# Attention output in split precision: one 128-column matmul a key chunk in place of three, with the parts added outside TensorE

## The chip, the cores and the metric

The kernel runs on one core of a Trainium2 chip. The metric is the device time in microseconds, taken as the median over runs. The core's engines are TensorE (PE, with its weight loads as PEld), VectorE (DVE), ScalarE (ACT), GpSimd (POOL) and SyncE (SP), which issues the transfers. Each engine works through its own instructions in program order and waits on semaphores for the others.

## The reference

A decoder with two layers works on x of shape (8, 100, 512) and a context of shape (8, 722, 512). Each layer has a mixing part, a cross attention over the context with 16 heads of 32 features, and a feed-forward part, each followed by a layer norm. The change touches the cross attention of both layers:

```python
q = split_heads(query @ Wq + bq)
k = split_heads(bank @ Wk + bk)
v = split_heads(bank @ Wv + bv)
scores = jnp.einsum('bhqd,bhkd->bhqk', q, k) / scale
attn = jax.nn.softmax(scores, axis=-1)
out = jnp.einsum('bhqk,bhkd->bhqd', attn, v)
out = out.transpose(0, 2, 1, 3).reshape(B, -1, D)
return out @ Wo + bo
```

The second layer's attention differs in having a mask over the keys and no biases on q, k and v. There are 8 batches, 100 queries (T) and 722 keys (KEYS) in each.

## The kernel before

Matmul operands are kept as two float32r parts, a high part and a low part that holds the rest, and each product is made by the helper `three` (lines 272 to 274): high by high, high by low, low by high, all added up in PSUM. ACT writes the high parts, DVE (or POOL) the low ones.

The keys of a batch are cut into six chunks of up to 128 (NKC = 6; the last has 82 rows). Attention handles one batch at a time, and within it one head a step: `batch` on PE runs steps t = 0 to 16, and DVE and ACT have a `batch` with the same steps. The order on each engine is written out by hand. In step t:

- PE: `scores(t)` into psS (one of two buffers), `transposes(t - 1)` of the exponentials into psT (a single buffer), then `weighted`, one half (three key chunks) of the product of probabilities and values for a pair of heads, into psO. In steps 0, 1, 4, 5, 8 and 9 it also projects a half of the next keys (`keys`), and in steps 15 and 16 those of the next batch.
- ACT: `probs_hi(t - 1)` (two copies of psT to pT.hi, line 615), then `exps(t)` (line 606), then whatever else the step has: a half of the keys (`keys_hi`), or in steps 10, 11, 13 and 14 the high part of the next batch's context (`context_hi`, line 565).
- DVE: `head_max(t)` (line 918; in the second layer lines 923 and 928), `probs_lo(t - 1)` (line 936), and in even steps from 4 on `heads_out` (line 947), which copies the two heads of a finished pair from psO to `oraw`.

The waits that tie the steps together: `exps(t)` waits for `head_max(t)`; `transposes(t)` waits for `exps(t)` and for `probs_lo(t - 1)`, as psT has one buffer; `weighted` of a pair waits for its low parts and for the `heads_out` of the pair before, as psO has one buffer. Steps 0 to 2 have no `weighted`.

Behind step 16 comes a tail: the values of the next batch (`values`, six times 12 matmuls) with the last pair's `weighted` between the first two of them, and on DVE the scaling of `oraw` by the reciprocal sums (line 978), in the first layer a bias (line 982), then the split into oT and the output projection. Below, "a step with keys" is one in which PE also runs `keys`.

## Time and profile before

| | |
|---|---|
| device time, median of 3 runs | 2616.84 us (2612.31 to 2621.23) |
| span of the profiled execution, first to last instruction | 2613.8 us |
| share of the span in which PE was busy | 93% |
| DVE, ACT, POOL | 42%, 36%, 22% |
| the chain that ended last, share on PE | 86% |
| mean granted TensorE clock | 0.934 |

The page gives the profiled execution by its span alone; the median of the runs is 3.0 us above it. The first layer's attention covers some 109 to 757 us of the span, the second layer's some 1131 to 1787. Matmul ends are modelled, so that PE's speed is read from the starts of successive matmuls and not from their durations. A wait is shown at the end of a row in brackets, with what ended it.

### The profile page before, as it was taken

To read this page: it belongs to the slowest core of one execution; us is meant where nothing else is said; L and a number is where in the kernel's file an instruction comes from. 1 tells how busy PE (TensorE), PEld (TensorE's weight loads), DVE (VectorE), ACT (ScalarE), POOL (GpSimd) and SP (SyncE) were. 2 spreads that over 40 slices of the span, in tenths; PEclk is the share of its full clock that TensorE was granted. 3 is DMA by queue.
4 is the path that set the end of the run, shared out by engine and by line. 5 is a ranking of instruction groups with operands and counts; after the bars stand their busy time and mean duration, and the time that the engine had idled before them with its cause. 6 is when DMAs were issued, how large, how long until landed. Compare 5 with 4: busy or idle time off the path is not lost.

```text
span 2613.8 us, 38193 instructions
## 1 busy us (share of the span) xinstructions
PE 2432.4 (93%) x14208; PEld 2160.2 (83%) x14208; DVE 1110.8 (42%) x2206; ACT 947.7 (36%) x1892; POOL 585.1 (22%) x397
## 2 busy tenths in 40 slices
PE   4899999999977789699999999998999999999997
PEld 3788888888866667588888888887999999999997
DVE  7455545555457368444556455654640000200022
ACT  2444434454443144343454344533222222311130
POOL 4111101110132634311111011101222222222222
PEclk9899999999978878789999999998999999999998
DMA  3000000000021010100100000000111111111111
GB/s 136 1 24 24 15 8 23 23 23 6 22 81 29 1 44 0 60 1 28 28 27 21 6 27 27 32 1 33 64 48 65 56 64 56 56 56 64 56 57 41
DMA packets 29513, 93.60 MB, mean 36 GB/s; under 512 B 3752, under 2 KB 4008, under 8 KB 29320
## 3 DMA queue, kind: packets, MB, share of 16 engines
q1 hardware_dynamic: 29448, 92.72, 11.0%
q8 instruction: 42, 0.69, 0.1%
q14 instruction: 23, 0.19, 0.0%
HBM read 91.07 MB, written 1.64 MB: 35 GB/s over the span
## 4 chain that ended last, share of the span: by engine, by line
PE 86%; DVE 6%; ACT 3%; POOL 3%; issue 2%; DMA 0%; DVEq 0%; SPq 0%; POOLq 0%; ACTq 0%
PE psS L272 18%; PE psS L274 16%; PE psS L273 16%; PE psT L1337 7%; PE psJ L272 4%; PE psJ L273 4%; PE psJ L274 4%; PE psO L272 4%; PE psO L274 3%; PE psO L273 3%; PE psT L272 2%; PE psT L274 2%; PE psT L273 2%; DVE x_res L884 1%; DVE stats L877 1%
## 5 line engine op out<-in xcount | busy, mean ns | idle before, releaser
L272 PE MATMUL psS<-hid_hi,fw_hi 128*128 128x400 f32 x1152 | 398.1, 346 | 15.4 <-DVE hid_lo L1258 10.6
L274 PE MATMUL psS<-hid_hi,fw_lo 128*128 128x400 f32 x1152 | 400.2, 347 | 0.0
L273 PE MATMUL psS<-hid_lo,fw_hi 128*128 128x400 f32 x1152 | 399.6, 347 | 0.0
L529 POOL TENSOR_TENSOR fw_lo<-raw,fw_hi 128x1024 fp32r<-128x1024 f32 x88 | 216.7, 2464 | 572.1 <-ACT fw_hi L751 572.1
L615 ACT ACTIVATE pT_hi<-psT 128x300 fp32r<-128x300 f32 x512 | 187.4, 418 | 263.0 <-PE psT L1337 262.5
L1258 DVE TENSOR_TENSOR hid_lo<-h_act,hid_hi 128x800 fp32r<-128x800 f32 x32 | 32.3, 1083 | 555.6 <-ACT hid_hi L840 555.6
L606 ACT ACTIVATE p<-psS,nmax 100x722 f32<-100x722 f32 x256 | 221.9, 867 | 68.9 <-DVE nmax L928 36.4
L936 DVE TENSOR_TENSOR pT_lo<-psT,pT_hi 128x300 fp32r<-128x300 f32 x512 | 216.4, 464 | 38.1 <-ACT pT_hi L615 32.8
L370 POOL TENSOR_TENSOR cT_lo<-ctx_raw,cT_hi 128x722 fp32r<-128x722 f32 x58 | 102.1, 1761 | 580.0 <-ACT cT_hi L565 580.0
L272 PEld LDWEIGHTS psS<-hid_hi,fw_hi 128*128 128x128 f32 x1152 | 218.0, 189 | 16.4 <-issue 11.2
L272 PE MATMUL psO<-pT_hi,vv_hi 128*64 128x200 f32 (+1 forms) x768 | 219.2, 285 | 2.4 <-DVE oraw L947 2.4
L272 PE MATMUL psJ<-cT_hi,wk_hi 128*128 128x362 f32 (+1 forms) x512 | 184.4, 360 | 38.3 <-POOL cT_lo L370 16.9
L274 PEld LDWEIGHTS psS<-hid_hi,fw_lo 128*128 128x128 f32 x1152 | 219.4, 190 | 0.0
L273 PEld LDWEIGHTS psS<-hid_lo,fw_hi 128*128 128x128 f32 x1152 | 218.0, 189 | 0.0
L1337 PE MATMUL psT<-ident,p 100*128 100x100 f32 x1536 | 198.6, 269 | 12.1 <-ACT p L606 12.1
L274 PE MATMUL psO<-pT_hi,vv_lo 128*64 128x200 f32 (+1 forms) x768 | 206.4, 269 | 0.0
L273 PE MATMUL psO<-pT_lo,vv_hi 128*64 128x200 f32 (+1 forms) x768 | 205.8, 268 | 0.0
L272 PE MATMUL psS<-kT_hi,qs_hi 32*100 32x512 f32 (+1 forms) x512 | 191.2, 373 | 4.6 <-POOL qs_lo L375 4.6
L1337 PEld LDWEIGHTS psT<-ident,p 100*128 100x128 f32 x1536 | 149.1, 147 | 42.9 <-DVE pT_lo L936 9.8
L273 PE MATMUL psJ<-cT_lo,wk_hi 128*128 128x362 f32 (+1 forms) x512 | 176.7, 345 | 0.0
L274 PE MATMUL psJ<-cT_hi,wk_lo 128*128 128x362 f32 (+1 forms) x512 | 175.8, 343 | 0.0
L273 PE MATMUL psS<-kT_lo,qs_hi 32*100 32x512 f32 (+1 forms) x512 | 169.3, 331 | 0.0
(306 smaller groups left out, 4909.4 us busy)
## 6 DMA issues: line engine op xcount, KB each, us to landing
raw<-ffn_dram SPq DMA_DIRECT2D x88, 512.0 KB, 3.2
ctx_raw<-ctxT_dram SPq DMA_DIRECT2D x60, 361.0 KB, 3.1
mask_raw<-mask_dram SPq DMA_DIRECT2D x8, 282.0 KB
raw<-wk_dram SPq DMA_DIRECT2D x4, 512.0 KB, 3.5
raw<-wv_dram SPq DMA_DIRECT2D x4, 512.0 KB, 6.6
raw<-wq_dram SPq DMA_DIRECT2D x4, 512.0 KB, 3.3
raw<-wo_dram SPq DMA_DIRECT2D x4, 512.0 KB, 3.2
cin<-xT_dram SPq DMA_DIRECT2D x1, 1600.0 KB, 8.3
```

Source lines behind the costliest of these rows:

```text
L272: nc.tensor.matmul(out, st[0], mv_[0], start=first, stop=False)
L273: nc.tensor.matmul(out, st[0], mv_[1], start=False, stop=False)
L274: return nc.tensor.matmul(out, st[1], mv_[0], start=False, stop=last)
L370: nc.gpsimd.tensor_tensor(cT.lo[:, c, :], src[:, c % 2, :], cT.hi[:, c, :], ALU.subtract)\
L529: nc.gpsimd.tensor_tensor(fw.lo[:, e, :], raw[:, e, :], fw.hi[:, e, :], ALU.subtract)\
L606: nc.scalar.activation(p[:, h % 2, 0:KEYS], psS[h % 2][0:T, 0:KEYS], ACT.Exp, bias=nmax[:, h % 2:h % 2 + 1], accum_out=rsum[:, h:h + 1]).t ...
L615: nc.scalar.activation(pT.hi[:, pr % 2, HK * i:HK * i + HK, (h % 2) * T:(h % 2 + 1) * T], psT[:, KA * i:KA * i + HK * T].rearrange("p (k t ...
L877: nc.vector.bn_stats(stats[:, s, :], src).then_inc(ln_stat, 1)
L884: nc.vector.tensor_scalar(x_res[:, b, :], src, mv[:, s, 0:1], rstd[:, s, :], ALU.subtract, ALU.mult).then_inc(ln_x, 1)
L936: nc.vector.tensor_tensor(pT.lo[sl], psT[:, KA * i:KA * i + HK * T].rearrange("p (k t) -> p k t", k=HK), pT.hi[sl], ALU.subtract).then_inc ...
L1258: nc.vector.tensor_tensor(hid.lo[:, k % M, :], h_act[:, k % M, :], hid.hi[:, k % M, :], ALU.subtract)\
L1337: mm = nc.tensor.transpose(psT[:, k0:k0 + T], p[:, h % 2, KC * k:KC * (k + 1)], ident[0:T, 0:T])
```

## The change

The two parts of the values, formerly two tensors, lie beside each other head by head in one tensor `vv`, so that for two heads 128 consecutive columns hold (head 0 high, head 0 low, head 1 high, head 1 low), 32 each. The two parts of the probabilities `pT` lie beside each other for each chunk, high for 2 x 100 queries and then low. One matmul a chunk multiplies all with all: 128 stationary columns, 400 moving ones. psO then holds every combination apart. What is wanted for head e is its rows of high values under the high and the low probabilities, and its rows of low values under the high ones. DVE adds the first two while it takes them out (a `tensor_reduce` over two elements in place of a copy), ACT copies the third to a new tensor `ocross` on the partitions of `oraw` (new `heads_cross`), and once a batch DVE adds `ocross` to `oraw`.

```diff
-        vv = pair("vv", [P, NKC, D])
+        vv = at("vv", [P, NKC, H, 2, HD], f32r)
...
-        pT = pair("pT", [P, 2, NKC, 2 * T])
+        pT = at("pT", [P, 2, NKC, 2, 2 * T], f32r)
...
+        ocross = at("ocross", [P, C, T], fp32)
...
+                def heads_cross(b, pr):
+
+                    act.wait_ge(a.pv_mm, H // 2 * b + pr + 1)
+                    if pr == 0:
+                        wait(act, a.o_summed, b)
+                    for e in range(2):
+                        g, j = divmod(2 * pr + e, G)
+                        cp = nc.scalar.activation(ocross[HD * j:HD * (j + 1), g, :],
+                                                  psO[2 * HD * e + HD:2 * HD * (e + 1), T * e:T * (e + 1)], ACT.Copy)
+                    cp.then_inc(a.o_crossed, 1)
...
                         if t < H:
                             exps(b, t)
+                        if t >= 4 and t % 2 == 0:
+                            heads_cross(b, (t - 4) // 2)
...
                         queries_hi(a, b + 1)
                         values_hi(a, b + 1, 0)
+                    heads_cross(b, H // 2 - 1)
+                    if not last:
                         values_hi(a, b + 1, 1)
...
                     for e in range(2):
                         g, j = divmod(2 * pr + e, G)
-                        cp = nc.vector.tensor_copy(oraw[HD * j:HD * (j + 1), g, :],
-                                                   psO[HD * e:HD * (e + 1), T * e:T * (e + 1)])
+                        r = slice(2 * HD * e, 2 * HD * e + HD)
+                        cp = nc.vector.tensor_reduce(oraw[HD * j:HD * (j + 1), g, :],
+                                                     psO[r, 0:4 * T].rearrange("p (s x t) -> p x t s", s=2, x=2)[:, e],
+                                                     AX.X, ALU.add)
...
+                    dve.wait_ge(a.o_crossed, H // 2 * (b + 1))
+                    dve.wait_ge(a.o_copied, H // 2 * (b + 1))
+                    nc.vector.tensor_tensor(oraw[:, :, :], oraw[:, :, :], ocross[:, :, :], ALU.add)\
+                      .then_inc(a.o_summed, 1)
                     dve.wait_ge(a.rb_mm, b + 1)
-                    dve.wait_ge(a.o_copied, H // 2 * (b + 1))
+                    dve.wait_ge(a.o_summed, b + 1)
...
                         wait(pe, a.o_copied, H // 2 * b + pr)
-                    fs = slice(2 * HD * pr, 2 * HD * (pr + 1))
+                        wait(pe, a.o_crossed, H // 2 * b + pr)
                     for k in range(HK * half, HK * (half + 1)):
                         n = key_rows(k)
-                        mm = three(psO[0:2 * HD, 0:2 * T], (vv.hi[0:n, k, fs], vv.lo[0:n, k, fs]),
-                                   (pT.hi[0:n, pr % 2, k, :], pT.lo[0:n, pr % 2, k, :]), k == 0, k == NKC - 1)
+                        mm = nc.tensor.matmul(psO[:, 0:4 * T],
+                                              vv[0:n, k, 2 * pr:2 * pr + 2, :, :].rearrange("p h s e -> p (h s e)"),
+                                              pT[0:n, pr % 2, k, :, :].rearrange("p s t -> p (s t)"),
+                                              start=k == 0, stop=k == NKC - 1)
```

What the change does to the instructions is seen in three places. The first is PE in a step without keys in the first layer: scores into psS, transposes into psT, then the half pair of `weighted` into psO (the last figure is rows of the output x moving columns). Before:

```order
L274 MATMUL psS<-kT_hi,qs_lo 100x512
L272 MATMUL psS<-kT_hi,qs_hi 100x210
L273 MATMUL psS<-kT_lo,qs_hi 100x210
L274 MATMUL psS<-kT_hi,qs_lo 100x210
L1337 MATMUL psT<-ident,p 128x100 x6
L272 MATMUL psO<-pT_hi,vv_hi 64x200
L273 MATMUL psO<-pT_lo,vv_hi 64x200
L274 MATMUL psO<-pT_hi,vv_lo 64x200
```

Now:

```order
L275 MATMUL psS<-kT_hi,qs_lo 100x512
L273 MATMUL psS<-kT_hi,qs_hi 100x210
L274 MATMUL psS<-kT_lo,qs_hi 100x210
L275 MATMUL psS<-kT_hi,qs_lo 100x210
L1360 MATMUL psT<-ident,p 128x100 x6
L1371 MATMUL psO<-pT,vv 128x400 x3
L273 MATMUL psS<-kT_hi,qs_hi 100x512
```

The last three rows of before stand twice more behind each other, and are not repeated. These nine matmuls of 200 columns into 64 rows became three of 400 columns into 128 rows; nothing else on PE moved. The second place is ACT in steps 10 to 12 of the first batch: exponentials of a head (p), the context's high part (cT_hi), the probabilities' high part (pT). Before:

```order
L606 ACTIVATE p,rsum<-psS,nmax 100x722
L565 ACTIVATE cT_hi<-ctx_raw 128x722
L615 ACTIVATE pT_hi<-psT 128x3x100 x2
L606 ACTIVATE p,rsum<-psS,nmax 100x722
L565 ACTIVATE cT_hi<-ctx_raw 128x722
L615 ACTIVATE pT_hi<-psT 128x3x100 x2
L606 ACTIVATE p,rsum<-psS,nmax 100x722
```

Now:

```order
L608 ACTIVATE p,rsum<-psS,nmax 100x722
L629 ACTIVATE ocross<-psO 32x100 x2
L566 ACTIVATE cT_hi<-ctx_raw 128x722
L617 ACTIVATE pT<-psT 128x3x100 x2
L608 ACTIVATE p,rsum<-psS,nmax 100x722
L566 ACTIVATE cT_hi<-ctx_raw 128x722
L617 ACTIVATE pT<-psT 128x3x100 x2
L608 ACTIVATE p,rsum<-psS,nmax 100x722
L629 ACTIVATE ocross<-psO 32x100 x2
```

The two copies stand behind the exponentials of every even step, and in step 10 (and 14) ahead of the context's part. The third place is DVE in the tail of the first batch, from the reciprocals on. Before:

```order
L969 RECIPROCAL rinv<-rsum 100x16
L908 TENSOR_TENSOR vv_lo<-psS,vv_hi 128x512 x2
L947 COPY oraw<-psO 32x100 x2
L908 TENSOR_TENSOR vv_lo<-psS,vv_hi 128x512
L978 TENSOR_TENSOR oraw<-psT,oraw 128x400
L982 TENSOR_TENSOR oraw<-oraw,cols 128x400
L908 TENSOR_TENSOR vv_lo<-psS,vv_hi 128x512
```

Now:

```order
L988 RECIPROCAL rinv<-rsum 100x16
L925 TENSOR_TENSOR vv<-psS,vv 128x16x32 x2
L965 TENSOR_REDUCE oraw<-psO 32x100 x2
L925 TENSOR_TENSOR vv<-psS,vv 128x16x32
L997 TENSOR_TENSOR oraw<-oraw,ocross 128x400
L1001 TENSOR_TENSOR oraw<-psT,oraw 128x400
L1005 TENSOR_TENSOR oraw<-oraw,cols 128x400
L925 TENSOR_TENSOR vv<-psS,vv 128x16x32
```

The addition of `ocross` stands ahead of the scaling, and the copies out of psO are reductions now, here as in every even step.

## Rows read from the trace of the kernel before

**Rows 1.** Page: the span, and the granted clock in 40 slices.

```profile
span 2613.8 us, 38193 instructions
...
PEclk9899999999978878789999999998999999999998
```

**Rows 2.** Windows over a batch: length, busy time of each engine, clock.

```profile
279.00:364.00 85.00, 84.40 (x526) 70.54 (x525) 43.96 (x87) 37.16 (x86) 10.08 (x8) 0.94 0.06 17
532.70:613.20 80.50, 79.90 (x526) 66.40 (x525) 44.08 (x87) 37.27 (x87) 10.10 (x8) 1.00 0.06 18
```

**Rows 3.** Timeline, second layer, a step without keys: start, length, engine, instruction.

```profile
1267.03 0.73 PE L1337 MATMUL psT<-ident,p 100*128 100x100 f32 x6
...
1267.29 0.92 DVE L923 CUSTOM_DVE_ANT_0 psS<-psS,maskb 100x722 f32<-100x722 f32 x1 [0.65 <-PE psS L274]
...
1267.54 0.31 PE L272 MATMUL psO<-pT_hi,vv_hi 128*64 128x200 f32 x1
...
1267.80 0.73 ACT L615 ACTIVATE pT_hi<-psT 128x300 fp32r<-128x300 f32 x2 [0.27 <-PE psT L1337]
...
1268.41 0.85 DVE L936 TENSOR_TENSOR pT_lo<-psT,pT_hi 128x300 fp32r<-128x300 f32 x2
...
1268.49 0.87 ACT L606 ACTIVATE p<-psS,nmax 100x722 f32<-100x722 f32 x1
...
1269.25 0.19 ACT L606 ACTIVATION_READ_ACCUMULATOR p<-psS,nmax 100x1 f32 x1
...
1269.29 0.52 DVE L947 COPY oraw<-psO 32x100 f32<-32x100 f32 x2
...
1269.69 0.73 PE L1337 MATMUL psT<-ident,p 100*128 100x100 f32 x6
```

**Rows 4.** Timeline of PE, second layer, the tail's six chunks of `weighted`, then `values`.

```profile
1279.26 0.25 PE L272 MATMUL psO<-pT_hi,vv_hi 128*64 128x200 f32 x1
...
1280.92 0.42 PE L272 MATMUL psS<-wv_hi,cT_hi 128*128 128x512 f32 x1
```

**Rows 5.** Timeline of PE, feed-forward, two matmuls that stand 20 apart.

```profile
2100.14 0.34 PE L272 MATMUL psS<-hid_hi,fw_hi 128*128 128x400 f32 x1
...
2103.78 0.34 PE L274 MATMUL psS<-hid_hi,fw_lo 128*128 128x400 f32 x1
```

**Rows 6.** Timeline of PE, first layer, `transposes(0)`, `transposes(1)`, then two chunks.

```profile
277.60 0.73 PE L1337 MATMUL psT<-ident,p 100*128 100x100 f32 x6
...
280.08 1.21 PE L1337 MATMUL psT<-ident,p 100*128 100x100 f32 x6 [0.60 <-ACT p L606]
...
281.59 0.37 PE L272 MATMUL psO<-pT_hi,vv_hi 128*64 128x200 f32 x1
...
282.09 0.37 PE L272 MATMUL psO<-pT_hi,vv_hi 128*64 128x200 f32 x1
```

**Rows 7.** Timeline of PE, second layer, the same two transposes of another batch.

```profile
1307.44 0.73 PE L1337 MATMUL psT<-ident,p 100*128 100x100 f32 x6
...
1309.98 0.73 PE L1337 MATMUL psT<-ident,p 100*128 100x100 f32 x6 [0.67 <-ACT p L606]
```

**Rows 8.** Single lines: count, shortest/median/longest in ns, first and last start.

```profile
L947 DVE COPY oraw<-psO x256: 237/254/260, 121.9 to 1778.7; 32x100 f32<-32x100 f32 x128
...
L1169 DVE TENSOR_REDUCE gsum<-gsq x8: 676/680/685, 946.1 to 1051.9; 100x16 f32<-100x512 f32 x8
...
L644 ACT ACTIVATE rT<-psT x16: 227/228/243, 169.6 to 1778.5; 16x100 f32<-16x100 f32 x16
...
L982 DVE TENSOR_TENSOR oraw<-oraw,cols x8: 574/575/576, 173.9 to 756.7; 128x400 f32<-128x400 f32 x8
```

**Rows 9.** Timeline of ACT, first layer, behind the context's part of step 10.

```profile
237.82 0.73 ACT L615 ACTIVATE pT_hi<-psT 128x300 fp32r<-128x300 f32 x2 [0.38 <-PE psT L1337]
```

**Rows 10.** Timeline of DVE, second layer, the tail, behind the scaling.

```profile
1291.53 0.69 DVE L908 TENSOR_TENSOR vv_lo<-psS,vv_hi 128x512 fp32r<-128x512 f32 x1 [2.90 <-ACT vv_hi L599]
```

**Rows 11.** Windows at the start of a batch, columns as in rows 2.

```profile
280.10:290.30 10.20, 10.20 (x46) 9.33 (x47) 3.04 (x6) 3.15 (x8) 0.00 (x0) 0.50 0.00 0
```

More of the change, by code:

```diff
@@ L232, in decoder_kernel @@
                               "qs_hi qs_done s_mm maxed exped t_mm pt_hi pt_lo pv_mm o_copied rinv_done rt_mm "
-                              "rt_copied rb_mm o_scaled "
+                              "rt_copied rb_mm o_scaled o_crossed o_summed "
                               "o_biased o_hi o_lo resid_done mask_in mask_done pad_done") for L in range(2)]
@@ L598, in values_hi @@
                 n = key_rows(j)
-                nc.scalar.activation(vv.hi[0:n, j, :], psS[j % 2][0:n, 0:D], ACT.Copy).then_inc(a.v_hi, 1)
+                nc.scalar.activation(vv[0:n, j, :, 0, :], psS[j % 2][0:n, 0:D].rearrange("p (h e) -> p h e", h=H),
+                                     ACT.Copy).then_inc(a.v_hi, 1)
             def attention(L):
@@ L615, in probs_hi @@
                         nc.scalar.activation(
-                            pT.hi[:, pr % 2, HK * i:HK * i + HK, (h % 2) * T:(h % 2 + 1) * T],
+                            pT[:, pr % 2, HK * i:HK * i + HK, 0, (h % 2) * T:(h % 2 + 1) * T],
                             psT[:, KA * i:KA * i + HK * T].rearrange("p (k t) -> p k t", k=HK), ACT.Copy)\
                           .then_inc(a.pt_hi, 1)
+                def heads_cross(b, pr):
[7 more added lines that the diff above has]
+                    cp.then_inc(a.o_crossed, 1)
                 def batch(b, last):
@@ L907, in values_lo @@
                 n = key_rows(j)
-                nc.vector.tensor_tensor(vv.lo[0:n, j, :], psS[j % 2][0:n, 0:D], vv.hi[0:n, j, :], ALU.subtract)\
-                  .then_inc(a.v_lo, 1)
+                nc.vector.tensor_tensor(vv[0:n, j, :, 1, :], psS[j % 2][0:n, 0:D].rearrange("p (h e) -> p h e", h=H),
+                                        vv[0:n, j, :, 0, :], ALU.subtract).then_inc(a.v_lo, 1)
             def attention(L, base):
@@ L934, in probs_lo @@
                         dve.wait_ge(a.pt_hi, 2 * (H * b + h) + i + 1)
-                        sl = (slice(None), pr % 2, slice(HK * i, HK * i + HK), slice((h % 2) * T, (h % 2 + 1) * T))
-                        nc.vector.tensor_tensor(pT.lo[sl],
+                        ks, ts = slice(HK * i, HK * i + HK), slice((h % 2) * T, (h % 2 + 1) * T)
+                        nc.vector.tensor_tensor(pT[:, pr % 2, ks, 1, ts],
                                                 psT[:, KA * i:KA * i + HK * T].rearrange("p (k t) -> p k t", k=HK),
-                                                pT.hi[sl], ALU.subtract).then_inc(a.pt_lo, 1)
+                                                pT[:, pr % 2, ks, 0, ts], ALU.subtract).then_inc(a.pt_lo, 1)
                 def heads_out(b, pr):
```

## The prediction, made before the changed kernel was run

> **What bounds the kernel now.** I read the page first: a span of 2613.8 us and a granted TensorE clock at or near full nearly everywhere [rows 1]. Attention is what the change touches, so I cut it into batches with the windows. A batch takes 85.0 us at a mean clock of 0.94, of which PE is busy 84.4; one batch takes 80.5 at clock 1.00, with the same 526 matmuls [rows 2]. DVE (44 us) and ACT (37) are busy for half of that. So PE bounds the batch as a whole, and the clock is worth some 4.5 us of it. The share of a batch is still an average, and what a shorter PE is worth must be read stage by stage.
>
> The timeline of a step without keys shows the other limit close by. From one set of transposes to the next is 1269.69 - 1267.03 = 2.66 us, and PE does not wait [rows 3]. But the exponentials that release the next transposes end at 1269.25 + 0.19 = 1269.44, only 0.25 us ahead of them. The reader is to see a ring: transposes, 0.77 later the high parts on ACT (1267.80), behind them the exponentials (1268.49), 0.95 to their end, and the next transposes. DVE has little room either: from its maximum at 1267.29 to the end of its copies at 1269.81 are 2.52 us in this even step.
>
> How fast the ring turns when PE is not in its way can be read off directly, in step 2, where PE has no `weighted` to do: transposes to transposes is 280.08 - 277.60 = 2.48 us in the first layer, with PE waiting 0.60 for ACT [rows 6], and 1309.98 - 1307.44 = 2.54 in the second, waiting 0.67 [rows 7]. I take these as the floor of a step.
>
> **What PE saves.** Six chunks of three 200-column matmuls take 1280.92 - 1279.26 = 1.66 us, 0.277 a chunk [rows 4]. A matmul of the new shape, 128 stationary by 400 moving columns, is the feed-forward's: twenty of them in 2103.78 - 2100.14 = 3.64 us, 0.182 each, weight loads hidden [rows 5]. That is 0.095 a chunk and 0.28 us a half pair of three chunks. Both prices are from long undisturbed runs of the same instruction forms, so the term is tight. The Trainium skill (VectorE: DVE Perf Modes, the TRN2 errata section) gives a matmul 6 cycles more than its columns; by that a chunk would save 0.088 us and the whole sum would be some 2 us smaller, and the rows above are slower than it for either shape.
>
> A batch has 16 half pairs: one in each of steps 3 to 16, and two in the tail.
>
> - PE is the bound in the steps with keys (4, 5, 8, 9, 15, 16) and in the tail. There all 0.28 comes out: 8 half pairs. A ninth is step 3, which stands in the stretch at half clock at the batch's start [rows 11], where PE is slower and so the bound: a chunk there takes 282.09 - 281.59 = 0.50 us [rows 6]. Its saving at that clock is larger (the new matmul costs at most twice 0.182, so 0.14 a chunk), but the stretch at half clock lasts as long as before and takes in other work instead, so I count it at 0.28. Sum 9 x 0.284 = 2.56 us.
> - Steps 6, 7, 10, 11, 12, 13 and 14 have no keys. PE would need 2.66 - 0.28 = 2.38, less than the floor. In the first layer they come down to 2.48 (0.18 each), in the second to 2.54 (0.12 each): 1.26 and 0.84 us.
>
> **What the additions cost.** *DVE*: a copy of 100 elements takes 0.254 us and a short-run reduction of 512 elements 0.680 [rows 8]. On the line between them (1.03 ns an element) the new reduction of 200 costs 0.36, so a pair goes from 0.52 to 0.72. The bounds are 0.254 (as the copy) and 0.68. The Trainium skill (VectorE: DVE Perf Modes, Rules for kernel authors) calls `tensor_reduce` the slowest DVE operation and advises against it on a hot path; by its "1x" the price is again one element a cycle, which the reduction's row agrees with, so it gives the same 0.36.
>
> Does DVE then bound the second layer? The chain over two steps, from one set of transposes: 0.77 to the high parts, some 0.42 for the first half of these, on which the low parts wait, 0.85 for the low parts, 0.72 for the reductions, 1.20 from the maximum's start to the exponentials' (1268.49 - 1267.29), 0.95 for these and some 0.15 for semaphores: 5.06 us [rows 3]. Two floors of 2.54 are 5.08. It is a tie, so I leave 2.54, but it has no slack: each 0.1 us more on a reduction lengthens a pair of steps by 0.2.
>
> *ACT*: two copies of 32x100 cost about as much as the 0.228 us of the nearest row [rows 8], 0.36 to 0.46 a pair. They stand behind the exponentials of even steps, where ACT otherwise idles until the next transposes (0.77 us are needed for them), so they are hidden. In steps 10 and 14 the context's part of the next batch is there too. ACT waited 0.38 us behind it at a step of 2.66 [rows 9]; at 2.48 some 0.20 is left, and 0.4 must fit in. I charge 0.2 twice a batch. If that cover were absent altogether, the copies would cost 0.4 in each of seven steps, 2.8 us a batch.
>
> The copies also stand in front of the next pair's `weighted`, as the reductions do: both end about when its transposes do. I charge nothing; the wait would take the place of the ring's.
>
> *Tail*: the addition of `ocross` is like the bias, 0.575 us [rows 8], and the last reductions 0.2. Behind the scaling DVE waits 2.90 us for the next batch's values [rows 10], and PE is busy with these. Hidden in seven batches; in the last batch of a layer nothing covers it, at most 0.8 us, 1.6 for both. I take 1. The new layouts of `vv` and `pT` have the same element counts and runs of 32 and 100 elements; I take no cost.
>
> **The sum.** First layer 2.56 + 1.26 - 0.40 = 3.42 us a batch, second 2.56 + 0.84 - 0.40 = 3.00; eight batches each: 27.4 + 24.0 = 51.4, less 1 for the ends of the layers: 50 us. Span 2613.8 - 50 = 2564; the runs' median stood 3.0 above the span, so 2567 us.
>
> **Rival 1: the clock falls more often.** At the start of a batch the clock goes to half for 10.2 us [rows 11], right after steps 1 and 2, in which PE did only 32-row scores and transposes and waited 0.60 us [rows 6]. One batch had the same wait and no fall [rows 2], so this stretch is near whatever decides. The change makes the steps without keys more like it: of 2.66 us they now spend 0.83 on `weighted`, afterwards 0.55 of 2.48 to 2.54, and PE waits 0.1 to 0.2 us in each; in steps 10 to 14 five of them stand in a row. If the clock falls there, for the same 10.2 us, it costs about what it costs now at the start, 4.5 us (85.0 - 80.5). Once a batch in the second layer: 36 us, leaving 14, 2603. The Trainium skill (TensorE: Matmul & The Clock Gate, What's actually happening) says that the clock follows how busy the array has been lately, which speaks for this rival. Against it: the new matmuls use all 128 columns and never leave PE idle for as much as 0.6. Chance 0.17.
>
> **Rival 2, the other side: the same fall in both layers.** Once a batch in 16 batches is 72 us against the 50 saved: 2639, slower. It decides from 0.7 falls a batch on. What speaks for it is that batches are alike, so that a fall that happens in one is likely to happen in most. Chance 0.14.
>
> **Rival 3: DVE or ACT becomes the bound.** With reductions of 0.5 us (the strided read of PSUM, two elements 200 apart, has no row), a pair of steps in the second layer is 5.06 + 0.28 = 5.34, as long as before (2 x 2.66), so that the 0.8 goes: 2573. At the upper bound of 0.68 it is 5.7: seven steps lose 0.19 each instead of gaining 0.12, in all 2.2 us a batch, and at most as much in the first layer: 35 us, 2602. Chance 0.13.
>
> **Rival 4: more than forecast.** If the matmul that fills the array keeps the clock up at the batch's start, 4.5 us in most of 16 batches comes on top: 2567 - 60 = about 2505; in part of them, 2540. Chance 0.1. That the change doesn't do what it says I exclude: the instruction order shows three matmuls where nine were.
>
> **How the numbers follow.** The forecast has 0.46: 2567, with a range of its own of 2552 to 2582 (floor of a step 0.1 lower or higher in 112 steps is 11 us, the ACT term 3, the tail 1). A measurement here tells some 0.3% from no change, 2609 to 2625. Faster: the forecast, rivals 3 and 4, and most of rival 1: 0.78. Slower: rival 2 with the upper half of what could come on top of it, 0.14. Within 0.3%: 0.08, from rival 1 with a few falls in the first layer too. The range must reach over rivals 3 and 1 and to the partial case of rival 4, and leaves out rival 2: 2543 to 2612.
>
> **What the profile would show.** The starts of two matmuls of line 1371 0.18 us apart at full clock. Transposes to transposes in steps 6 to 14 without keys 2.48 in the first and 2.54 in the second layer, now with a wait of PE for ACT. Line 965 at 0.36 us, line 629 at 0.23. A batch at 81.5 us in the first layer with one stretch at half clock. A second such stretch in steps 10 to 14 would show rival 1 or 2; a PE wait for the maximum of DVE, or a longer line 965, rival 3. The prediction is wrong if the steps with keys do not shorten by 0.28, or if the clock does something else than before.

## The result: 61 us slower, where 50 us faster was forecast

The changed kernel takes 2679.51 us (median of 4 runs, 2664.34 to 2687.57), the kernel before beside it 2618.20 us (4 runs, 2612.31 to 2621.23). The ratio is 1.0225 [1.0189, 1.0261]. Here and below medians are over all runs of a kernel and ratios over its fast runs alone, so that the two can differ where the runs spread. The forecast was 2567 with a range of 2543 to 2612; what came is rival 2, and more of it than its 2639.

The page of the changed kernel (profiled run 2664.34 us), for [rows 1]:

```profile
span 2662.5 us, 35459 instructions
...
PE 2463.9 (93%) x12672; PEld 2144.8 (81%) x12672; DVE 1148.7 (43%) x2222; ACT 1012.1 (38%) x2148; POOL 583.6 (22%) x397
...
PEclk9789899879888778788889898988999999999998
```

PE is as busy as before, 93%, with 1536 matmuls fewer. The clock row tells why: in attention (slices 3 to 12 and 18 to 28) there are 8s and 7s in most places where 9s were. The mean granted clock went from 0.934 to 0.897. The windows of one whole batch of the first layer, of a row of its steps at full clock, and of the steps behind it:

```profile
281.67:369.93 88.26, 86.77 (x430) 69.94 (x429) 46.27 (x88) 41.44 (x101) 10.05 (x8) 0.86 0.06 17
...
303.94:325.60 21.66, 21.00 (x129) 16.61 (x129) 15.61 (x31) 15.05 (x38) 3.18 (x2) 1.00 0.04 7
325.60:339.30 13.70, 13.70 (x52) 11.30 (x51) 6.52 (x13) 7.37 (x20) 3.77 (x3) 0.50 0.32 98
```

A batch has 96 matmuls fewer than in [rows 2] and takes 88.3 us in place of 85.0, at a clock of 0.86. Beside the stretch at half clock at its start [rows 11] it has a second one, of 13.7 us, in steps 12 to 15. Stretches are counted here and below in the trace's record of the granted clock: those that begin between the first transposes of a layer's attention and 12 us behind its last ones. There are 15 before (143 us) and 32 after (341 us).

What the change costs on the other engines, single lines, for [rows 8] (line 965 is the reduction, 629 ScalarE's copy):

```profile
L965 DVE TENSOR_REDUCE oraw<-psO x256: 343/360/367, 128.7 to 1827.1; 32x100 f32<-32x200 f32 x128
...
L629 ACT ACTIVATE ocross<-psO x256: 242/246/250, 124.6 to 1827.0; 32x100 f32<-32x100 f32 x128
```

The first is as forecast, 0.36 us. The second is a little longer, 0.246 us for 0.23, and a pair of copies takes 0.50 (below) where 0.36 to 0.46 was forecast. What both do to the steps was not forecast. Three places of the timeline show it; in each row the figures are start and length. First ScalarE in the step of the first layer in which a part of the context stands behind the copies, for [rows 9]:

```profile
320.37 0.50 ACT L629 ACTIVATE ocross<-psO 32x100 f32<-32x100 f32 x2
...
320.48 0.73 PE L1360 MATMUL psT<-ident,p 100*128 100x100 f32 x6
...
320.90 0.81 ACT L566 ACTIVATE cT_hi<-ctx_raw 128x722 fp32r<-128x722 f32 x1
...
321.73 0.73 ACT L617 ACTIVATE pT<-psT 128x300 fp32r<-128x300 f32 x2
...
323.44 0.73 PE L1360 MATMUL psT<-ident,p 100*128 100x100 f32 x6 [0.46 <-ACT p L608]
```

Transposes to transposes is 323.44 - 320.48 = 2.96 us, 0.48 over the floor of 2.48; 0.2 was charged. Second a step with keys: DVE has the keys' low part to do first, so the reductions start with the next transposes and the next pair's first matmul waits for their end at 314.08 (the profile names no releaser for it, "issue"):

```profile
312.85 0.59 DVE L917 SCALAR_TENSOR_TENSOR kT_lo<-psJ,cols,kT_hi 128x362 fp32r<-128x362 f32 x1 [1.88 <-ACT kT_hi L591]
...
313.29 0.73 PE L1360 MATMUL psT<-ident,p 100*128 100x100 f32 x6
313.36 0.72 DVE L965 TENSOR_REDUCE oraw<-psO 32x100 f32<-32x200 f32 x2
...
314.14 0.48 PEld L1371 LDWEIGHTS psO<-pT,vv 128*128 128x128 f32 x3 [0.31 <-issue]
```

Third a pair of steps without keys in the second layer, for [rows 3]. It runs from the transposes at 1358.71 to those at 1364.07, 5.36 us, where 5.08 was forecast and before it was 2 x 2.66 = 5.32:

```profile
1358.71 0.73 PE L1360 MATMUL psT<-ident,p 100*128 100x100 f32 x6
...
1359.48 0.73 ACT L617 ACTIVATE pT<-psT 128x300 fp32r<-128x300 f32 x2 [1.35 <-PE psT L1360]
...
1360.09 0.85 DVE L953 TENSOR_TENSOR pT<-psT,pT 128x300 fp32r<-128x300 f32 x2
...
1360.97 0.74 DVE L965 TENSOR_REDUCE oraw<-psO 32x100 f32<-32x200 f32 x2
...
1361.73 0.92 DVE L940 CUSTOM_DVE_ANT_0 psS<-psS,maskb 100x722 f32<-100x722 f32 x1
...
1362.98 0.86 ACT L608 ACTIVATE p<-psS,nmax 100x722 f32<-100x722 f32 x1 [0.22 <-DVE nmax L945]
...
1364.07 0.47 PE L1360 MATMUL psT<-ident,p 100*128 100x100 f32 x3 [0.32 <-ACT p L608]
```

DVE goes from low parts to reductions to maximum without a gap, and ScalarE waits for the maximum: VectorE is the bound there. These are steps 6 and 7; in steps 12 and 13 of the same layer, at full clock in only two batches, a pair takes some 2.47 + 2.59 = 5.06.

### The profile page after: what moved, and what is told of

Read it like the earlier page. It is cut to its first block, busy times and chain, and to the rows that moved or that the text cites. A ratio compares the mean times of both kernels' runs of the same rounds, so it can differ in the third digit from the quotient of the medians.

```text
span 2662.5 us, 35459 instructions
## 1 busy us (share of the span) xinstructions
PE 2463.9 (93%) x12672; PEld 2144.8 (81%) x12672; DVE 1148.7 (43%) x2222; ACT 1012.1 (38%) x2148; POOL 583.6 (22%) x397
## 4 chain that ended last, share of the span: by engine, by line
PE 81%; DVE 8%; ACT 5%; issue 3%; POOL 3%; DMA 0%; DVEq 0%; SPq 0%; POOLq 0%; ACTq 0%
PE psS L273 17%; PE psS L275 16%; PE psS L274 16%; PE psT L1360 7%; PE psO L1371 6%; PE psJ L273 4%; PE psJ L274 4%; PE psJ L275 4%; PE psT L273 2%; PE psT L275 2%; PE psT L274 2%; ACT p L608 1%; DVE x_res L901 1%; DVE stats L894 1%; ACT pT L617 1%
## 5 line engine op out<-in xcount | busy, mean ns | idle before, releaser
L617 ACT ACTIVATE pT<-psT 128x300 fp32r<-128x300 f32 x512 | 187.5, 418 | 272.8 <-PE psT L1360 271.6
L1371 PE MATMUL psO<-pT,vv 128*128 128x400 f32 (+1 forms) x768 | 240.2, 432 | 4.5 <-DVE oraw L965 2.5
L953 DVE TENSOR_TENSOR pT<-psT,pT 128x300 fp32r<-128x300 f32 x512 | 216.3, 464 | 65.0 <-ACT pT L617 62.0
L1360 PE MATMUL psT<-ident,p 100*128 100x100 f32 x1536 | 222.4, 290 | 23.2 <-ACT p L608 21.7
L1360 PEld LDWEIGHTS psT<-ident,p 100*128 100x128 f32 x1536 | 167.7, 162 | 61.5 <-DVE pT L953 22.6
L273 PE MATMUL psS<-kT_hi,qs_hi 32*100 32x512 f32 (+1 forms) x512 | 204.3, 399 | 4.6 <-POOL qs_lo L376 4.6
L274 PE MATMUL psJ<-cT_lo,wk_hi 128*128 128x362 f32 (+1 forms) x512 | 184.4, 360 | 0.0
L275 PE MATMUL psS<-kT_hi,qs_lo 32*100 32x512 f32 (+1 forms) x512 | 181.9, 355 | 0.0
L274 PE MATMUL psS<-kT_lo,qs_hi 32*100 32x512 f32 (+1 forms) x512 | 181.4, 354 | 0.0
L273 PEld LDWEIGHTS psS<-kT_hi,qs_hi 32*100 32x100 f32 x512 | 90.8, 177 | 100.4 <-issue 68.9
```

The costliest lines, as they stand in the source:

```text
L273: nc.tensor.matmul(out, st[0], mv_[0], start=first, stop=False)
L274: nc.tensor.matmul(out, st[0], mv_[1], start=False, stop=False)
L275: return nc.tensor.matmul(out, st[1], mv_[0], start=False, stop=last)
L617: nc.scalar.activation(pT[:, pr % 2, HK * i:HK * i + HK, 0, (h % 2) * T:(h % 2 + 1) * T], psT[:, KA * i:KA * i + HK * T].rearrange("p (k t ...
L953: nc.vector.tensor_tensor(pT[:, pr % 2, ks, 1, ts], psT[:, KA * i:KA * i + HK * T].rearrange("p (k t) -> p k t", k=HK), pT[:, pr % 2, ks, ...
L1360: mm = nc.tensor.transpose(psT[:, k0:k0 + T], p[:, h % 2, KC * k:KC * (k + 1)], ident[0:T, 0:T])
```

## The experiments

Two theories stood at the start. **A**: the clock falls because matmul work in the steps without keys has become thin, and TensorE waits in them. **B**: the time went to the additions on DVE and ScalarE, the clock being as before. Each ratio below is to the kernel before, timed beside it, with its 95% interval. "Stretches" are those at half clock in both attentions, counted as above in the trace of one execution; where the runs of a kernel spread, the count is that of this one.

### More matmul work: idle matmuls in the steps without keys

`e1_fill_two` puts an idle matmul behind each of the first two chunks of a half pair, `e1_fill_four` two of them, into columns of psO that nothing reads:

```diff
+                        if k % HK < HK - 1 and 2 * pr + 3 + half in (6, 7, 10, 11, 12, 13, 14):
+                            for i in range(FILL_N[k % HK]):
+                                nc.tensor.matmul(psO[:, 4 * T:KA], <vv, 128 columns>, <vv, 112 columns>,
+                                                 start=False, stop=False)
```

> The changed kernel with two idle matmuls (128 stationary by 112 moving columns, into psO columns nobody reads) added to each half pair of weighted in steps 6, 7 and 10 to 14. Theory A (the half clock in steps 10 to 14 comes from TensorE having too little to do there): work is added and the kernel gets faster; the stretch at half clock in steps 10 to 14 shrinks or is gone, which is worth up to 6.8 us a batch; 2575 to 2640. Theory B (the loss is the work added on ACT and DVE, and the clock falls because PE waits for them): the steps stay as long, the clock falls as before, 2675 or some more.

> As e1_fill_two with four idle matmuls in each half pair of those steps, some 0.2 to 0.34 us a step. Theory A: no half clock in steps 10 to 14 in nearly all batches; the steps are 2.5 to 2.7 us again, a batch some 82.5 us, 2575 to 2595. Theory B: 2675 or more.

Two gave 2600.29 us, 0.9925 [0.9899, 0.9951], four 2609.85, 0.9976 [0.9950, 1.0002], above the 2575 to 2595 expected of them: twice the idle work does not gain twice. With two, work was added and 79 us went away. The steps without keys became longer (2.62 us for 2.48), but the stretches fell from 32 to 15 (126 us), and none begins in steps 10 to 13. That is theory A. The Trainium skill (TensorE: Matmul & The Clock Gate, A second HAM failure mode: psum-queue depth-cycling) describes a kernel in which frequent short idling between groups of matmuls makes the clock go up and down; by that rule the fill should help, and the trace agrees (15 stretches for 32).

### Less matmul work without the rest of the change

`e2_light_before` is the kernel before without the product of the values' low and the probabilities' high parts, which it leaves out; six matmuls of 200 columns a half pair take the place of nine.

```diff
-                        mm = three(psO[0:2 * HD, 0:2 * T], (vv.hi[...], vv.lo[...]), (pT.hi[...], pT.lo[...]), ...)
+                        nc.tensor.matmul(psO[0:2 * HD, 0:2 * T], vv.hi[0:n, k, fs], pT.hi[0:n, pr % 2, k, :], ...)
+                        mm = nc.tensor.matmul(psO[0:2 * HD, 0:2 * T], vv.hi[0:n, k, fs], pT.lo[0:n, pr % 2, k, :], ...)
```

> The kernel before with the product of the low values and the high probabilities left out in weighted: two matmuls of 200 columns a chunk (0.184 us, as the one of 400), nothing added on ACT or DVE, and so a less exact output. Theory A: steps 10 to 14 get a stretch at half clock as in the changed kernel, and the kernel is slower than before though it does less: 2640 to 2690. Theory B: no such stretch, 2560 to 2570. If only 64 stationary columns or 128 mattered to the clock, this and e3 would differ.

`e3_no_extract` is the changed kernel with new matmuls, but copies in place of reductions, and without ScalarE's copies and the addition; it leaves out the two mixed products.

> The changed kernel with the additions on ACT and DVE taken out: DVE copies the high by high part alone, ACT takes out nothing, no sum at the end, so the output lacks the low parts. Matmuls as in the changed kernel. Theory A: the half clock in steps 10 to 14 stays, time within 15 us of the changed kernel's 2680. Theory B: it goes, 2560 to 2570.

They took 2553.05 (0.9757 [0.9720, 0.9794]) and 2566.75 (0.9781 [0.9716, 0.9847]). So less matmul work alone does not bring the clock down, and theory A in its plain form fell: but for the last batch of the first layer, where the kernel before has one too, `e2_light_before` has no stretch in the middle of a batch, and `e3_no_extract` has them in four batches of the second layer and none in the first. The four runs of `e3_no_extract` are two near 2551 us and two near 2581, and its trace is of one of the latter (2582.06). Its steps without keys in the first layer are the forecast's 2.48, or 2.55 (step 7).

### Which of the additions

`e5_copies_alone` adds ScalarE's copies to `e3_no_extract`, `e6_reduce_alone` the reductions. Each leaves out what the other does, and the addition of `ocross`. Theory C in their expectations is that it takes both the shorter matmul work and the one longer wait, 0.46 us behind the copies in step 11.

> Of the additions on ACT and DVE only ACT's two copies a pair: DVE copies the high by high part as before, and there is no sum, so the output lacks the low parts. Theory C: step 10 to 11 is 2.9 us again, and the half clock is back in both layers: 2640 to 2690. If DVE's reductions made the loss: near e3_no_extract, 2567.

> Of the additions only DVE's reductions in place of its copies; ACT takes out nothing and there is no sum, so the output lacks the product of the low values. Theory C: the first layer has no half clock in steps 10 to 14; in the second layer, where DVE's chain of two steps (5.06 us) ties with the ring, a few more than in e3_no_extract: 2565 to 2600. If the reductions made the loss: 2640 or more.

The copies gave 2599.79 (0.9919 [0.9892, 0.9947]), the reductions 2658.85 (1.0154 [1.0112, 1.0196]). The copies cost 33 us over 2566.75, between the two times expected of them. The larger part, against theory C of the expectation, is the reductions: 92 us over 2566.75. The fourth case tells what they cost with the old matmuls. In `g2_before_reduce` the kernel before reduces over the two column halves of psO (the wrong columns are added):

```diff
-                        cp = nc.vector.tensor_copy(oraw[HD * j:HD * (j + 1), g, :], psO[HD * e:HD * (e + 1), T * e:T * (e + 1)])
+                        cp = nc.vector.tensor_reduce(oraw[HD * j:HD * (j + 1), g, :],
+                                                     psO[HD * e:HD * (e + 1), 0:2 * T].rearrange("p (s t) -> p t s", s=2),
+                                                     AX.X, ALU.add)
```

> The kernel before with VectorE's two copies of a pair replaced by reductions over two elements (the two column halves of psO, so that the wrong columns are added and the output is not the reference's). It is the fourth case beside old matmuls with copies (the kernel before, 2618), new matmuls with copies (2567) and new matmuls with reductions (2659). If the longer VectorE chain alone brings the clock down, it loses as much as there: 2680 to 2710. If it takes both, thin matmul work and longer waits (theory A), it loses only what the steps with keys lose, 0.2 us in two of them a batch, and little of the clock: 2620 to 2640.

2632.98 us, 1.0044 [1.0025, 1.0063]: 13 us. The four cases are the main result of the study:

| | copies on DVE | reductions on DVE | difference |
|---|---|---|---|
| old matmuls | 2619.6, 15 stretches | 2633.0, 16 stretches | 13 |
| new matmuls, nothing else | 2566.8, 21 stretches | 2658.9, 29 stretches | 92 |

The clock rows of the pages, `g2_before_reduce`:

```profile
PEclk9899999999988878789999999998999999999998
```

and `e6_reduce_alone`:

```profile
PEclk9889998888878878788888889888999999999998
```

Neither thin matmul work nor a longer DVE chain brings the clock down much by itself; the two together do.

How small the waits are that the reductions make shows in the first layer of `e6_reduce_alone`. Its steps there differ from those of `e3_no_extract` in 5 and 9 alone, where PE waits 0.1 and 0.2 us ahead of `weighted`, and five of its batches get a second stretch all the same. One of them, windows of the 11 us before it and of its larger part:

```profile
562.40:573.40 11.00, 10.96 (x65) 8.60 (x66) 8.15 (x16) 8.05 (x19) 3.21 (x2) 1.00 0.09 20
573.50:587.10 13.60, 13.60 (x51) 11.22 (x50) 6.38 (x13) 6.16 (x15) 3.63 (x3) 0.50 0.32 89
```

PE was busy for 10.96 of 11.00 us, and then the clock fell. So it is not the length of a wait in the thin steps that decides. How waits of up to 0.2 us that lie 6 to 12 us back come to matter, these runs do not show.

### Length of the steps, and what the clock costs

A step here runs from the first transpose of `transposes(k - 1)` to that of `transposes(k)`; medians of the batches at full clock, from the starts in the traces. The columns e3 to g1 are the runs whose names begin so:

| step, layer | before | after | e3 | e5 | e6 | g2 | g1 (below) |
|---|---|---|---|---|---|---|---|
| 5, first (keys) | 4.76 | 4.69 | 4.48 | 4.49 | 4.71 | 4.97 | 4.69 |
| 9, first (keys) | 4.80 | 4.72 | 4.56 | 4.52 | 4.78 | 5.01 | 4.73 |
| 8, first (keys) | 4.66 | 4.40 | 4.39 | 4.39 | 4.39 | 4.66 | 4.39 |
| 6, first | 2.66 | 2.48 | 2.48 | 2.48 | 2.48 | 2.66 | 2.62 |
| 11, first | 2.66 | 2.96 | 2.48 | 2.96 | 2.48 | 2.66 | 2.83 |
| 15, first (keys) | 3.41 | - | 3.15 | 3.81 | 3.15 | 3.41 | 3.67 |
| 7, second | 2.65 | 2.81 | 2.60 | 2.60 | 2.81 | 2.70 | 2.74 |

The reductions take 0.2 us in steps 5 and 9 of both layers, and in steps 7 and 11 of the second. ScalarE's copies take 0.48 in step 11 and 0.66 in step 15 of the first layer. The prediction charged 0.2 for each. How the last comes about is seen in `e5_copies_alone`, ScalarE, POOL and PE at the end of step 14:

```profile
413.12 0.50 ACT L629 ACTIVATE ocross<-psO 32x100 f32<-32x100 f32 x2
...
413.23 0.73 PE L1354 MATMUL psT<-ident,p 100*128 100x100 f32 x6
...
413.65 0.81 ACT L566 ACTIVATE cT_hi<-ctx_raw 128x722 fp32r<-128x722 f32 x1
...
414.63 1.75 POOL L371 TENSOR_TENSOR cT_lo<-ctx_raw,cT_hi 128x722 fp32r<-128x722 f32 x1 [1.40 <-ACT cT_hi L566]
...
416.44 0.43 PE L273 MATMUL psJ<-cT_hi,wk_hi 128*128 128x362 f32 x1 [0.40 <-POOL cT_lo L371]
```

The copies hold the context's last part, that holds its low part on POOL, and the next keys wait for it.

The runs give the price of the clock too, as each lists its span and its mean clock. Time at half clock is 2 x (1 - clock) x span. Within a kernel, over 106 runs of the changed kernel and the 18 experiments, each microsecond more at half clock goes with 0.39 us more of device time (correlation 0.99; 0.32 to 0.50 in single kernels). The Trainium skill (TensorE: Matmul & The Clock Gate, Terms) would make it 0.5; the runs give less, perhaps as PE would have waited for part of that time anyway. With 0.39:

| | device time | at half clock | the rest (time - 0.39 x half) |
|---|---|---|---|
| before (59 runs) | 2619.6 | 356 | 2481 |
| after | 2679.5 | 594 | 2448 |
| e3_no_extract | 2566.8 | 364 | 2425 |
| e5_copies_alone | 2599.8 | 416 | 2438 |
| e6_reduce_alone | 2658.9 | 550 | 2444 |

So the change saves 33 us outside the clock, and the clock costs 0.39 x 238 = 93 us: 60 us in all, and 61 were measured. This split is an estimate from that slope, and moves with it; the times do not.

### The wait behind the copies

`e4_context_nine` moves the context's first part to step 9, where no copies stand: `CONTEXT_AT = {9: 0, 11: 1, 13: 2, 14: 3}`.

> The changed kernel, complete, with one number changed: ACT makes the first context part of the next batch in step 9 (behind the keys' half) and not in step 10. Step 10 then holds the two copies alone, so the 0.46 us wait of PE ahead of the transposes of head 10 goes. Theory C (the half clock of steps 10 to 14 needs both, less matmul work and this one longer wait): the stretch at half clock in steps 10 to 14 goes from the first layer and from most of the second; 2560 to 2600. Theory A' (less matmul work alone): it stays in most batches, 2640 or more.

2646.89 us, 1.0115 [1.0099, 1.0132]: 33 us less than after, of which step 11 accounts for some 4 (7 x 0.48 in the first layer, where it comes down to 2.48, and 7 x 0.14 in the second, to 2.81). 27 stretches are left. That is outside the 2560 to 2600 of theory C: the long wait in step 11 is not what the second stretch needs. `f4_accumulate` and `f5_accumulate_nine` avoid the reductions (DVE copies; ScalarE's copies and the addition stay) and compute the whole result:

```diff
-                        mm = nc.tensor.matmul(psO[:, 0:4 * T], <vv, 128 columns>,
-                                              pT[0:n, pr % 2, k, :, :].rearrange("p s t -> p (s t)"), ...)
+                        for s in range(2):
+                            mm = nc.tensor.matmul(psO[:, 0:2 * T], <vv, 128 columns>, pT[0:n, pr % 2, k, s, :], ...)
```

> The changed kernel with the matmul of 400 columns cut into two of 200 that add up in the same PSUM columns (values' parts stationary as before, first the probabilities' high part, then the low one). The sum over the two column halves then exists already, and DVE copies 32x100 in place of reducing; ScalarE's copies and the addition of them stay. The whole result is computed (the product of the two low parts is added too). Theory A+reduction (the reductions lengthen the steps and, with the waits that they make, bring the clock down): close to the kernel with ScalarE's copies alone, 2590 to 2610. Rival (the block of 128 stationary columns itself, or the separate matmuls, cost what was lost): 2640 or more.

> The kernel f4_accumulate with the first part of the next batch's context moved from step 10 to step 9, so that it no longer stands behind ScalarE's copies in step 10. Theory A: the step of 2.96 us comes down to 2.5, the stretches at half clock in the middle of a batch mostly go; 8 us from the step and up to 25 from the clock: 2565 to 2595. Rival (the clock does not depend on that wait): 8 us less than f4_accumulate, no fewer stretches.

`f4_accumulate` took 2630.98 (1.0037 [1.0016, 1.0058]), above its expectation: two matmuls of 200 are not as short as one of 400, a step with keys takes 4.51 for 4.39. `f5_accumulate_nine` took 2657.77 (1.0148 [1.0106, 1.0189]), 27 more than with the wait. Its six runs spread from 2619 to 2668, and two of them lie among the ten of `f4_accumulate` (2620 to 2641), so that the size of the loss is uncertain; that nothing was gained is not. Both misses count against the simple picture that each wait taken away helps the clock. The same edit gained 33 us in one kernel and none in the other.

### The start of a batch

`e7_fill_start_before` gives the kernel before three idle matmuls of 128 x 384 ahead of `transposes(1)` in step 2.

> The kernel before with three idle matmuls (128 stationary by 384 moving columns, 0.55 us, into psO while nothing is in it) ahead of transposes(1) in step 2, in the 0.60 us that PE waits there. If the fall of the clock at the start of each batch comes from TensorE having too little to do, it goes and saves up to 4.5 us in some 14 batches: 2555 to 2575. If not, 2620.

2606.79 us, 0.9955 [0.9937, 0.9973]. They stood one step too early. The transposes that wait in [rows 6] and [rows 7] are `transposes(2)` of step 3; the text ahead of the prediction calls them `transposes(1)`, one too low. Step 1 became 0.62 us longer, and only part of the stretches went (10 are left). `f2_fill_third_before` has them in the right place:

```diff
                     for t in range(H + 1):
                         if t < H:
                             scores(b, t)
+                        if t == 3:
+                            wait(pe, a.o_copied, H // 2 * b)
+                            for i in range(3):
+                                nc.tensor.matmul(psO[:, 0:384], vv.hi[:, 0, 0:P], vv.hi[:, 1, 0:384], start=True, stop=True)
                         if t >= 1:
                             transposes(b, t - 1)
```

> The kernel before with three idle matmuls of 128 by 384 columns (into psO, never read) in front of the transposes of step 3, where TensorE waits 0.60 to 0.67 us for the exponentials; the earlier run with the same three put them one step too early, in front of a step that had no wait, where they lengthened step 1 by 0.62 us. Theory A (the clock falls where matmul work is thin and TensorE waits): the half-clock stretch at the start of most batches goes or shortens, the step stays at 2.48 to 2.54, and up to 60 us are saved: 2555 to 2590. Rival (the stretch at the start is decided elsewhere, by the tail of the batch before): no change, 2612 to 2625.

2580.76 us, 0.9843 [0.9809, 0.9878]: 39 us off the kernel before. The step stays at 2.48, so the idle work lies wholly in the wait. In place of 10.2 us most stretches at a batch's start last 3.4 us, or are gone (9 stretches, 51 us).

### Both fills, and useful work in place of idle work

`g1_after_fills` is the changed kernel with the fill of `e1_fill_two` and that of step 3; `h1_after_fill_third` has the latter alone; `h2_after_fills_nine` is g1 with the context in step 9; `f6_accumulate_all` is `f5_accumulate_nine` with both fills.

> The changed kernel with both kinds of idle matmuls: two of 128 by 112 columns a half pair in steps 6, 7 and 10 to 14 (2600 alone), and three of 128 by 384 in front of the transposes of step 3 (they took 39 us off the kernel before). Theory A: 2600 less 25 to 40, 2560 to 2575. Rival (the two do not add, since the start of the batch is thinner with the new matmuls in steps 3 to 5): 2585 or more.

> The changed kernel with the three idle matmuls of 128 by 384 columns in front of the transposes of step 3 and no other. If the stretch at the start and the one in the middle of a batch are two things: 2679 less 30 to 40, 2640 to 2650, and the stretches in steps 10 to 15 stay. If the second follows from the first: most of the 117 us of both fills, 2565 to 2600, and few stretches in the middle.

> The changed kernel with both kinds of idle matmuls and the context's first part in step 9. The step from 10 to 11 takes 2.83 us in the first layer and 2.90 in the second there, and should come down to some 2.62 and 2.75: 14 times 0.2 us, 2562 less 3, 2556 to 2562, if the clock holds as it did. Rival (the shift of the work costs clock, as it did in f5_accumulate_nine): 2575 or more.

> The kernel f5_accumulate_nine with two idle matmuls of 128 by 112 columns a half pair in steps 6, 7 and 10 to 14, and three of 128 by 384 in front of the transposes of step 3. Theory A: both kinds of stretches at half clock go, steps without keys stand at some 2.6 us: 2530 to 2570, faster than every kernel so far. Rival (the idle work costs its length and the clock does not repay it): 2590 or more.

`g1_after_fills` takes 2562.04 us (2556.38 to 2565.27), 0.9763 [0.9734, 0.9792]: 58 us less than before and 117 less than the changed kernel, with its full result. Windows of a batch in either layer, to hold against the 88.26 us above:

```profile
273.72:352.90 79.18, 78.30 (x448) 63.47 (x447) 46.32 (x88) 41.51 (x101) 10.09 (x8) 1.00 0.07 19
1270.50:1349.60 79.10, 78.43 (x447) 63.52 (x446) 48.61 (x119) 41.22 (x101) 12.79 (x9) 1.00 0.08 22
```

Such a batch is 1.3 us shorter than the one at full clock of [rows 2], and now most are like it (7 stretches, 65 us). By the estimate above the rest is 2454, so it is slower than the changed kernel outside the clock (2448) and wins by the clock alone. That holds a kernel with idle work against one without: against the kernel before with the fill of step 3 (2580.76) the gain is 19 us, and that kernel was not run with idle work in other steps. `h1_after_fill_third` lies between, 2623.97 (0.9910 [0.9876, 0.9943]), its ten runs from 2584 to 2647, on both sides of the kernel before; its trace (2634.73) has 22 stretches, some in steps 6 and 7 too. So the fill at the start does not stop those in the middle, and neither of its two expectations was met. With this fill in both, the changed kernel is still 43 us slower by the medians (2623.97 for 2580.76). `h2_after_fills_nine` gives 2561.59, 0.9776 [0.9737, 0.9814], as its expectation had it, and no different from g1 within the spread. `f6_accumulate_all` gives 2588.90, 0.9857 [0.9812, 0.9901], above its expectation of 2530 to 2570; its steps without keys take 2.72, more than before.

`g3_hybrid` keeps the three old matmuls, with copies and nothing on ScalarE, for pairs 4 and 5 (steps 11 to 14), and has the context's first part in step 9; `g4_hybrid_fill` adds the fill of step 3.

```diff
+                        if pr in (4, 5):
+                            mm = three(psO[0:2 * HD, 0:2 * T], (vv[0:n, k, pr, 0, :], vv[0:n, k, pr, 1, :]),
+                                       (pT[0:n, pr % 2, k, 0, :], pT[0:n, pr % 2, k, 1, :]), k == 0, k == NKC - 1)
+                            continue
```

> The changed kernel with pairs 4 and 5 (steps 11 to 14, heads 8 to 11) in the old form, three matmuls of 200 columns into 64 rows, a copy on VectorE, nothing on ScalarE; the other six pairs in the new form; the context's first part in step 9. The values lie by pairs (both heads' high parts, then both heads' low parts). Theory A (useful matmul work in the row of thin steps holds the clock): no stretch at half clock in steps 10 to 15, mechanical gain 1 to 2 us a batch against the kernel before: 2585 to 2605. Rival (the new form in steps 3 to 10 and its reductions already bring it down): 2620 or more.

> g3_hybrid with the three idle matmuls of 128 by 384 columns in front of the transposes of step 3. Theory A: g3_hybrid less 30 to 40, 2545 to 2575, below the kernel before with the same fill (2581). Rival: no better than 2581.

`g3_hybrid` took 2645.47 us (1.0078 [1.0040, 1.0116]): useful work in steps 11 to 14 does not hold the clock. In its trace (a run of 2674.74) the stretches start earlier, in step 10 or at the first 0.1 us of step 11, so that what brought them on lies before step 11, in steps of the new form. `g4_hybrid_fill` took 2572.76 (0.9798 [0.9767, 0.9829]), 8 us less than the old form with the same fill, and 73 less than `g3_hybrid`, where 30 to 40 were expected. Its trace has 7 stretches for 25: here a fill at the start took away most of those in the middle too.

## Why the prediction was wrong

**What PE saves: right.** 0.095 us a chunk gives 9 x 0.284 us a batch and the floors, 57.7 us before any cost. `e3_no_extract`, which has the saving and no additions, has 56 us less outside the clock (2481 - 2425, by the slope above), and its steps without keys stand at 2.48 to 2.55 in the first layer and 2.44 to 2.60 in the second. The 2 us by which the other price of a chunk would have made the sum smaller are 3 by its own figures (0.007 in 27 chunks and 16 batches); nothing hangs on it. That it came out at the forecast's 2567 is chance: its additions are absent and its clock is a little worse.

**What the additions cost: 7 us charged, 23 measured** (2448 - 2425). The prices of single instructions were nearly right; wrong was how much idle time there was to hide them. "I charge nothing; the wait would take the place of the ring's" fails where there is no ring wait, in the steps with keys: 0.2 us twice a batch. The chain of DVE in steps 6 and 7 of the second layer, "5.06 us", is 5.36: low parts start 0.61 us after the high parts' start, not 0.42, as they stand behind the maximum ([rows 3] had that 0.61 already, 1268.41 - 1267.80), and some 0.1 more lies between the links. "It is a tie" was wrong by 0.28 there. That is the length of rival 3's first case, 5.34, but not by its cause: the reductions took their 0.36. "I charge 0.2 twice a batch" came out at 0.48 and 0.66 in the first layer. The pair of copies takes 0.50 us, not 0.4, and for step 14 the chain was not followed from ScalarE over POOL to the keys. ([rows 9] is the row behind the context's part of step 13; behind that of step 10 ACT waited 0.43 us at a step of 2.70, which leaves the same 0.2.)

**The clock: the step that failed.** The sum has no term for a second stretch at half clock, and the reason given is this: "Against it: the new matmuls use all 128 columns and never leave PE idle for as much as 0.6." In the thin steps the waits were indeed no longer than 0.5 us, and the clock fell all the same, once more in nearly every batch of both layers. Rival 2 named place and number; its chance of 0.14 was too low, since one argument, the longest single wait, was held against a second stretch, and that length does not decide: in `e6_reduce_alone` second stretches came after waits of no more than 0.2 us. Its size was off too: the long ones among the second stretches last 13.7 to 20.5 us, not 10.2. So 93 us, not 72, against 33, not 50.

**Rival 4** did not come by itself: the stretch at the start stayed, in all 16 batches for 13 before. That it was worth having is shown by `f2_fill_third_before`.

**What stays open.** That the thin matmul work and the longer DVE chain together bring the clock down is shown by the four cases, and that more matmul work in the thin steps brings it back by the fills. That the chain does it by way of PE's waits is only argued. What exactly decides in a batch is not: with the context in step 9 one kernel gained 33 us and another nothing, `e2_light_before` and `e3_no_extract` have nearly the same steps in both layers, and in the second only the one with the wide matmuls has stretches in the middle (in the trace of a run of 2582 us), and equal batches of one run go both ways. A batch's length shifts when the next one's thin steps come; that may decide, and no run here tested it.

## What to carry to other kernels

Where TensorE bounds a kernel, a saving there is worth only what it is after the engines beside it and the clock have had their part: work out for each freed stretch whether TensorE will wait in it, and treat a row of steps with little matmul work beside short waits as a risk to the clock, even if no wait is long. Add up a chain over engines with the order of the instructions in it, and ask of each engine what it does just before the link. When a change saves matmul time and the page's clock row sinks, put idle matmuls into the waits before giving the change up: here that turned 61 us slower into 58 us faster. Give the old form the same help before comparing: it gained 39 us from one fill, and against that the change with both fills is 19 us faster.

## What the runs showed of the hardware

- The granted clock fell to half (1.2 of 2.4 GHz) where the longest wait of TensorE was 0.46 us: between 320.48 and 325.60 of the changed kernel it ran transposes, wide matmuls and 32-row scores almost without a break, waited 0.46 us once, and was at half speed for the next 13.7 us, in which it had no wait at all. In `e6_reduce_alone` it fell at 573.47 after 11 us of which TensorE was busy 10.96.
- Stretches at half clock in the attentions lasted 3.4 to 27.3 us in these runs.
- A microsecond more at half clock went with 0.39 us more of device time (0.32 to 0.50 in single kernels).
- Two matmuls of 200 columns into 128 rows in place of one of 400 make a half pair of three chunks 0.12 us longer (a step with keys 4.51 for 4.39), though they move the same columns.
- A reduction of two elements 200 apart out of PSUM (32x100 results) took 0.36 us, a copy of 32x100 0.25 on VectorE and on ScalarE alike.
